# A graph network layer on one core: the node layer of each sum, and the skip layer, in the edge loop

## What is computed

```
h    = relu(layernorm(x))                        # 12500 x 128
sc   = h @ sc weights * node_attr                # skip layer, per node
lin  = h @ lin1 weights * node_attr              # per node
w    = mlp(rbf(dist) * cut(dist))                # 200000 x 128: 8 -> 64 -> 64 -> 128
msg  = tensor_product(w, lin[src], edge_attr)    # 200000 x 256
agg  = segment_sum(msg, dst) / max(count, 1)     # 12500 x 256
l2   = agg @ lin2 weights * node_attr            # 12500 x 128
alpha= tanh(agg @ alpha_w * node_attr)
out  = x + sc + alpha * l2
```

## Time and profile before

| | us |
|---|---|
| median of 3 runs | 2159.24 (2158.75 to 2160.36) |
| the profiled execution | 2159.53 |
| its span, first to last instruction | 2157.6 |
| stage 1, up to the first gather | 110.9 |
| edge loop, first gather to last L1017 | 1969.5 |
| stage 3 and its barrier, from there to the end | 77.2 |

### The profile page before, as it was taken

How to read it: one execution, slowest core, us unless ns; L and a number is a source line. 1 busy time by engine, 2 the same in 40 slices (tenths; PEclk the granted TensorE clock), 3 DMA queues, 4 the chain that set the end, 5 groups by cost and what they waited for, 6 DMA issues and landing times. The chain is left out here.

```text
span 2157.6 us, 33815 instructions
## 1 busy us (share of the span) xinstructions
PE 1692.3 (78%) x7419; PEld 1337.9 (62%) x7419; DVE 1621.2 (75%) x3574; ACT 863.7 (40%) x2388; POOL 1589.6 (74%) x1730
## 2 busy tenths in 40 slices
PE   3867877778777787777877778777787777877778
PEld 2656666666666666666666666666666666666668
DVE  8667777777777777777777777777777777777767
ACT  4733333333333333333333333333333333333345
POOL 7677777777777777777777777777777777777734
PEclk9989999999999999999999999999999999999999
DMA  4922222222222222222222222222222222222249
GB/s 148 274 68 56 56 56 56 55 55 56 56 56 55 55 56 56 56 55 55 56 56 56 55 55 56 56 56 56 55 57 56 56 55 55 57 56 56 56 112 266
DMA packets 249202, 152.25 MB, mean 71 GB/s; under 512 B 145591, under 2 KB 222960, under 8 KB 249184
## 3 DMA queue, kind: packets, MB, share of 16 engines
q0 software_dynamic: 50112, 102.73, 18.3%
q1 hardware_dynamic: 199072, 49.33, 10.3%
HBM read 130.23 MB, written 21.66 MB: 70 GB/s over the span
## 5 line engine op out<-in xcount | busy, mean ns | idle before, releaser
L808 POOL DMA_INDIRECT lin_g<-lin_table,src_ix x1566 | 1480.3, 945 | 487.5 <-issue 487.5
L862 PE MATMUL ps_agg<-msg,onehot 128*128 128x257 f32 x3132 | 742.9, 386 | 236.6 <-DVE agg L1017 236.6
L862 PEld LDWEIGHTS ps_agg<-msg,onehot 128*128 128x128 f32 x3132 | 573.3, 190 | 389.8 <-issue 315.8
L855 PE MATMUL ps_w<-w,h 128*128 128x256 f32 x1566 | 424.8, 407 | 165.4 <-ACT h L908 163.6
L919 ACT ACTIVATE lin_sh<-lin_g,meta 128x128 f32<-128x128 f32 x1566 | 486.0, 389 | 161.5 <-DMA lin_g<-lin_table,src_ix 160.6
L855 PEld LDWEIGHTS ps_w<-w,h 128*128 128x128 f32 x1566 | 336.3, 253 | 300.4 <-ACT h L908 283.7
L983 DVE TENSOR_TENSOR lin_sh<-lin_g,ps_meta 128x576 f32<-128x576 f32 x261 | 196.8, 754 | 422.9 <-DMA lin_g<-lin_table,src_ix 422.8
L901 ACT ACTIVATE h<-ps_h 128x384 f32<-128x384 f32 x261 | 126.7, 486 | 713.7 <-PE ps_h L838 713.7
L988 DVE TENSOR_TENSOR onehot<-iota,ps_meta 128x768 f32<-128x768 f32 x261 | 246.4, 944 | 0.0
L838 PE MATMUL ps_h<-rbf,w 128*128 128x192 f32 x1044 | 214.2, 328 | 3.4 <-DVE rbf L974 3.4
L846 PE MATMUL ps_h<-h,w 128*128 128x384 f32 x522 | 212.3, 489 | 0.0
(11 more groups left out here) (130 smaller groups left out, 981.0 us busy)
## 6 DMA issues: line engine op xcount, KB each, us to landing
lin_g<-lin_table,src_ix POOLq DMA_INDIRECT x1566
xq<-in_x SPq DMA_DIRECT2D x24, 256.0 KB, 3.8
lin_table<-node_out SPq DMA_DIRECT2D x24, 256.0 KB, 3.4
sc_table<-node_out SPq DMA_DIRECT2D x24, 256.0 KB, 3.7
x<-in_x SPq DMA_DIRECT2D x24, 256.0 KB, 3.5
sc<-sc_table SPq DMA_DIRECT2D x24, 256.0 KB, 4.4
out_dram<-new SPq DMA_DIRECT2D x24, 256.0 KB, 3.2
src_ix<-in_src SPq DMA_DIRECT2D x268, 3.0 KB, 1.6
```

Source lines behind the costliest of these rows:

```text
L808: pool.indirect_dma_start(lin_g[:, u, j, :], None, lin_table, bass.IndirectOffsetOnAxis(ap=src_ix[:, u, j:j + 1], axis=0)).then_inc(gather ...
L855: mm = pe.matmul(ps_w[:, 2 * j * P:(2 * j + 2) * P], cols[:, j, :], w3[:], start=True, stop=True)
L862: mm = pe.matmul(ps_agg[:, 0:COLS], onehot[:, u % 2, j, :], msg[:, u % 2, j, :], start=(j == 0), stop=(j == TILES - 1))
```

## The change

- **Stage 2, node layer in the loop.** segment_sum now takes the messages as the stationary operand and the one-hot tile as the moving one: twelve products of 128 columns in place of six of 257, and the sum comes out transposed (ps_sumT). ACT copies it (copy_sums, at the head of each of its steps). PE applies lin2 and alpha to it (node_layer, two accumulated products of 129 columns) and multiplies the edge count with a one. DVE counts edges by a reduction over the one-hot tiles (counts, 768 elements) and accumulates 130 columns instead of 257, one group later and inside `late`, between the messages o11 and o01. The two blocks of `agg` shrink likewise.
- **Stage 2, skip layer in the loop.** In iterations 0 to 48 PE multiplies two blocks of hT with w_sc, ACT scales them, DVE adds x (skip_sum, 256 columns) into an SBUF tile `skip`; SP loads the two operands after a wait for the skip_sum before.
- **Stage 2, the quotient.** cut/dist is no longer formed in stage 1. DVE forms it once an iteration (quotient: a reciprocal of 16x192 and a product) at the end of step u=3; spread_aq at the head of the next step waits for it.
- **Stage 1.** x is loaded first and the statistics start at once; the preparations are spread over the steps; the weights' DMAs are issued by ACT, 28 of them ahead of its first root; rstd is no longer applied by POOL but by ACT as it evacuates. sc_table is gone; hT is stored instead (the same bytes). L644 and the later q product are gone.
- **Stage 3.** One chain forms count, gain and tanh for all nodes at once; then three blocks of a step are scaled and added by DVE, the fourth by ACT and POOL, and the step is stored. No loads, no PE.

The core of the diff:

```
@@ PE, stage 2 @@
 def spread_aq(i):
-    pe.wait_ge(aq_in, 64 * (i + 1))
+    pe.wait_ge(quot_ready, i + 1)
...
-    pe.matmul(ps_rbf[:, 1, 0:SEG], sel_one[:], aq[:, 1, :], start=True, stop=True).then_inc(rbf_spread, 1)
+    pe.matmul(ps_rbf[:, 1, 0:SEG], sel_one[:], quot[:], start=True, stop=True).then_inc(rbf_spread, 1)
...
-def segment_sum(i, u):
+def segment_sum(i, u, skip_pair=None):
+    n = i * SLOTS + u
+    if skip_pair is not None:
+        pe.wait_ge(hT_landed, 16 * (skip_pair + 1))
+        for b in range(2):
+            pe.matmul(ps_sc[:, b * P:(b + 1) * P], hT_in[:, b * P:(b + 1) * P], w_sc[:], start=True, stop=True)
     pe.wait_ge(msg_ready, i * SLOTS + u + 1)
-    pe.wait_ge(agg_ready, i * SLOTS + u + 1)
-    for j in range(TILES):
-        mm = pe.matmul(ps_agg[:, 0:COLS], onehot[:, u % 2, j, :], msg[:, u % 2, j, :], ...)
+    for c in range(2):
+        for j in range(TILES):
+            mm = pe.matmul(ps_sumT[:, c * P:(c + 1) * P], msg[:, u % 2, j, c * P:(c + 1) * P], onehot[:, u % 2, j, :], ...)
     mm.then_inc(sums_ready, 1)
+def node_layer(i, u):
+    n = i * SLOTS + u
+    pe.wait_ge(count_ready, n + 1)
+    pe.wait_ge(sumT_ready, n + 1)
+    pe.wait_ge(w_read, ... n + 2)
+    pe.wait_ge(agg_ready, n + 1)
+    pe.matmul(ps_l2[:, COUNT:COLS], edge_count[:, u % 2, :], one[:], start=True, stop=True)
+    for c in range(2):
+        mm = pe.matmul(ps_l2[:, 0:COUNT], sumT[:, u % 2, c * P:(c + 1) * P], w_lin2[:, c, :], ...)
+    mm.then_inc(l2_ready, 1)
...
 for u in range(SLOTS):
     if u == 0:
         spread_aq(i + 1)
+    node_layer(the group before)
     layer3(i, u + 1)
     segment_sum(i, u)            # layer1, layer2 follow as before
@@ ACT, stage 2 @@
+    copy_sums(i, u)
+    if share and u == 1:
+        scale_sc(...)
     if u == 0:
         sines(i + 1)
@@ DVE, stage 2 @@
+def quotient(i):
+    dve.wait_ge(aq_in, 64 * (i + 1))
+    at_least(dve, rbf_spread, i)
+    dve.reciprocal(quot[:], aq[:, 0, :]).then_inc(recip_done, 1)
+    dve.wait_ge(recip_done, i + 1)
+    dve.tensor_tensor(quot[:], quot[:], aq[:, 1, :], ALU.mult).then_inc(quot_ready, 1)
...
 for u in range(SLOTS):
-    late(i + (u + 1) // SLOTS, (u + 1) % SLOTS)
+    late(i + (u + 1) // SLOTS, (u + 1) % SLOTS, earlier)     # accumulate(earlier) ahead of o01
+    counts(i + (u + 1) // SLOTS, (u + 1) % SLOTS)
     if u == 0:
         fractions(i + 1)
     products(*ahead)
-    accumulate(i, u)
     columns(*ahead)
     if u == 0:
         basis(i + 1)
+    if u == 2 and share:
+        skip_sum(i, ...)
+    if u == 3 and not last:
+        quotient(i + 2)
```

More of the change, by code:

```diff
@@ L109, in window_steps, with blocks @@
     def window_steps(b):
-        return sum(7 if padded(k) else 6 for k in range(b))
+        return sum(5 if padded(k) else 4 for k in range(b))
+    def blocks(n):
+        return NB if n < STEPS else REST
     def parted(table):
@@ L210, in gnn_kernel @@
[L210 to L214, removed]
@@ L265, in _ @@
[L265 to L273, removed]
@@ L274, in _ @@
[L274 to L277, removed]
-                    sp.dma_start(w_lin2[0:HID, 0, 0:MUL], lin2_ws).then_inc(w_edges_in, 16)
-                    sp.dma_start(w_lin2[0:HID, 0, DIM:], alpha_w).then_inc(w_edges_in, 16)
+                    load_x(2)
@@ L450, in product, with turn @@
-                    def product(t, j, blocks=NB):
-                        n, b = t * UNROLL + j, j % 2
+                    def turn(n):
+                        if n <= STEPS:
+                            pe.wait_ge(h_ready, n + 1)
+                            at_least(pe, hT_ready, n - 1)
+                            for k in range(blocks(n)):
+                                last = pe.transpose(psT[:, n % 2, k * P:(k + 1) * P], h[:, n % 2, k, :], ident[:])
+                            last.then_inc(transposed, 1)
@@ L1138, in _ @@
-                    for i in range(IN):
-                        load(i, i)
-                    steps(sp, body)
-                    for b in range(2):
-                        whole = len(range(b, STEPS, 2))
-                        sp.wait_ge(out3[b], 16 * (whole + (REST if b == STEPS % 2 else 0)))
+                    for n in range(STEPS):
+                        sp.wait_ge(low_ready, n + 1)
+                        sp.wait_ge(high_ready, n + 1)
+                        sp.dma_start(node_rows(out, n), result[:, n * NB:(n + 1) * NB, :]).then_inc(out_stored, 16)
@@ L1185, in _ @@
                     dve.wait_ge(scale_ready, 1)
-                    copy_low(0, 0)
-                    steps(dve, body)
-                    update(STEPS, STEPS % IN)
+                    dve.tensor_tensor(pre[:], whole[:, :, ALPHA], scale[:], ALU.mult).then_inc(pre_ready, 1)
+                    dve.wait_ge(alpha_ready, 1)
+                    dve.tensor_tensor(gain[:], alpha[:], scale[:], ALU.mult).then_inc(gain_ready, 1)
+                    dve.wait_ge(gain_ready, 1)
+                    for n in range(STEPS + 1):
+                        for j in range(min(ON_DVE, blocks(n))):
+                            blk, rows = n * NB + j, slice(0, P if n < STEPS else REST_ROWS[j])
+                            last = dve.scalar_tensor_tensor(out=result[rows, blk, :], in0=whole[rows, blk, 0:DIM], scalar=gain[rows, blk:blk + 1],
+                                                            in1=result[rows, blk, :], op0=ALU.mult, op1=ALU.add)
+                        last.then_inc(low_ready, 1)
@@ L1251, in _ @@
+                    act.wait_ge(pre_ready, 1)
+                    act.activation(alpha[:], pre[:], ACT.Tanh).then_inc(alpha_ready, 1)
+                    act.wait_ge(gain_ready, 1)
+                    for n in range(STEPS):
+                        blk = n * NB + ON_DVE
+                        at_least(act, high_ready, n - 1)
+                        act.activation(grown[:, n % 2, :], whole[:, blk, 0:DIM], ACT.Copy, scale=gain[:, blk:blk + 1]).then_inc(grown_ready, 1)
                 @block.gpsimd
```

947 lines of the change are left out of this document (443 added, 504 removed).

## The result

| | before | after |
|---|---|---|
| median (range), us | 2159.78 (2158.75 to 2160.36) | 2460.78 (2458.33 to 2461.51) |
| span | 2157.6 | 2457.7 |
| stage 1, to the first gather | 110.9 | 112.0 |
| loop, to the last accumulate | 1969.5 | 2312.9 |
| stage 3 | 77.2 | 32.8 |

The ratio is 1.139 (95% interval 1.137 to 1.141). The forecast was 2263, its range 2175 to 2345: the direction and the place are right, the time is 198 us too low. By stages the loop cost 343 instead of 168, stage 1 gained nothing instead of 16, stage 3 gained 44 instead of 48.

What follows compares the result with a forecast made beforehand. POOL's issuing of gathers, 30.0 us an iteration, was taken to set the loop's pace. From 2159.5 us, +168 for the loop (45 of it clock), -16 for stage 1 and -48 for stage 3 gave 2263; range 2175 to 2345.

Steps and rivals of the forecast that it cites:

- The added wait: Loop, after the quotient: DVE and PE wait in turn through spread_aq, node_layer and layer3, 3.40 us once an iteration.
- The register load: DVE's step in the loop: no longer hidden behind L983, it costs 0.15 us a group, bounds 0 and 0.68.
- The 0.35 at u=0: Loop, step u=0: late waits on ACT's sine and scale_lin; 0.35 us taken of a computed 0.46.
- The reciprocal: DVE's quotient, once an iteration: reciprocal of 192 columns at 6.0 ns a column, 1.33 us.
- PE's 24 short products: segment_sum on PE in the loop: 24 x 0.116 = 2.78 us, against 2.85 for 12 products of 257 columns.
- rival 4: Weight loads of a group's 24 short products aren't hidden: 250 us more in the loop, total 2510; chance 0.05.
- The clock: TensorE's half clock after idling for the quotient: 0.7 us an iteration, bounds 0 and 1.5, 45 us in all.
- rival 1: Half clock after every quotient on all of the chain: 96 us in place of 45, total 2314; chance 0.18.
- The counts: DVE's reduction of 768 one-hot elements in each group: 0.92 us, bounds 0.67 and 1.1.
- Stage 1: Earlier start, first store near 22 instead of 40: 94 against 110.9 us; -16 taken, bounds -5 and -28.
- Stage 3: After the loop: DVE adds three blocks a step at 0.27 us each; about 29 us against 77.2, so -48.
- Rival 2: The wait is covered and POOL stays the loop's bound: loop +2, total 2098, faster; chance 0.09.

Runs made afterwards that it cites:

- e13: Changed kernel plus 32 TensorE products of 128 columns, read by nothing, after layer2 of step u=3; 3240.2 us beside 3129.9 of the kernel before.
- e9: Changed kernel, quotient at end of u=1, POOL normalising with ones and zeros columns (mean not subtracted); 2101.02 us beside 2161.74 of the kernel before.
- e5: Changed kernel with only quotient(i+2) moved from the end of step u=3 to u=1; 3097.1 us against 3177.2 of the kernel before.

## Why the prediction was wrong, step by step

- **The added wait** was right: place, order, both engines in turn, 3.40 us at full clock (3.30 in e13). The register load was sized 0.15 and costs nothing, its lower bound: o11 (L1041) starts at 1010.83, the accumulate at 1011.10, 0.27 behind it. The 0.35 at u=0 is a wait of 0.25. The reciprocal was 1.33 as worked out, PE's 24 short products 2.68 from start to start (2.78 worked out), so rival 4 falls.
- **The clock** is one of the two mis-sized terms. The step said that three us at half speed cost 1.5 us of work and took 0.7. Both halves failed. The bound asked how much work is lost in 3 us, but the chain has 3.3 us of work at full clock and takes nearly twice that at half: 2.65 more. And the row it was read from, the stretch at 0.50 that began 1.7 us after PE resumed, came after an idle time of 2.97; here PE idles 5.12 us and the clock had in nearly every stop fallen before it resumed, in the one shown 2.5 us before. 64 x (2.65 - 0.7) = 125 us. Even rival 1, which had the clock pay every time, priced it at 1.5. The Trainium skill (TensorE: Matmul & The Clock Gate, HAM oscillation) says that idle gaps in a loop bring the half clock in every turn; the trace agrees, with 0.50 to 0.55 over the chain behind each of the 64 quotients.
- **The counts** were scaled by elements from a reduction whose inner step is 128 bytes: 0.72 for 576, so 0.92 for 768. Measured 1.40, with a step of 512 bytes, beyond my upper bound of 1.1. That alone is 64 x 4 x 0.48 = 123 us, as much as the clock. The register load's 0.15 and some 0.06 elsewhere came back, so a group's step was 6.53 in place of 6.26, 64 x 4 x 0.27 = 69 us. The row was of the right operation and nearly the size, but of another stride; the Trainium skill (SBUF — State Buffer, Door 1: The DMA port swizzle) says that each access that crosses into another line of 16 bytes pays, but gives no price. By that rule 128 and 512 bytes would cost the same; here they are 1.40 and 1.92 ns an element, against 1.23 for neighbours (the reduction at 1.40 takes three elements into one, the two others six, so it differs in more than the stride).
- Together the iteration adds up to 4 x 6.53 + 0.91 + 0.33 + 1.71 + 5.95 + 0.25 = 35.3, and from k_turn to k_turn it is 35.4 (with a skip pair). Without the clock's 2.65 and the stride's 2.0 it would be 30.7. That both gains would show in the time is arithmetic, no run has it. The two missed terms, 125 and 69, less 19 are the loop's 175: the wait at u=0 was 0.10 smaller (6), the chain at full clock 3.30 and not 3.40 (6), the stops average 5.89 and not 5.95 (4), and start and end, with what the last iteration saves, cost 6 and not 9 (3).
- **Stage 1**: I worked out ACT's queue (first store 24.6, predicted 22) and the bytes, but kept POOL's four operations a step at their price before, though their form changed. With 0.71 instead of 0.44, POOL bounds the stage: 112.0 instead of 94. With the cheap form it is 94.1 to 92.0, near the predicted value. 18 us.
- **Stage 3**: blocks cost 0.33 instead of 0.27 on DVE, 4 us.
- **The range** ended at 2345 by less than its own bounds. The register load's 0.53 in three or four steps of 64 iterations is 102 to 136 us and not 70, and the upper bound of the counts, 1.1 for 0.92, another 46, which the range left out.
- **Rivals.** Rival 1's condition came true, half clock after every quotient, at nearly twice its price. Rival 2 didn't come true in this kernel, but by e9 an early quotient gives what it named, POOL as the bound, at 2101 (2098 worked out). DVE alone needs 4 x 6.53 + 0.91 + 0.33 + 1.71 = 29.1 us, less than POOL's 30.0 even with the dear counts.

## What to carry to other kernels

Ask of each value that one engine hands to another in an in-order queue how long before its use it can be made: here the loop lost 343 us with two instructions at the end of one step and 3 us with the same two, two steps earlier. When a chain on TensorE runs after an idle time like the 5.12 us here, price all of it at half clock, not part of it by what a row elsewhere shows. Take an instruction's price only from a row with the same operation, stride and operand form, and recheck each engine that a stage's new bytes and queues leave nearest its limit.

## What the runs showed of the hardware

- DVE's reduction of 768 float32 elements to 128: 0.94 us over neighbours, 1.47 over elements 512 bytes apart.
- POOL's operation on 128x128 float32: product and sum of two columns 0.45 us (median), subtraction and maximum or sum with a number 0.71, subtraction and maximum with a column 0.79.
- TensorE's granted clock fell to half (1.2 GHz) around each idle time of 5.12 us in the loop, 2.0 to 5.3 us after the last product, and came back 4.8 to 8.2 us after PE had resumed; it stayed at 1.00 in the stop of e13 shown above, where 64 instructions had filled most of the wait. A chain of 3.30 us took 5.95 at half.
- A register load from SBUF on DVE, behind instructions that ran without a wait, cost nothing: the accumulate behind it started 0.27 after the instruction before it. In the kernel before it cost 0.27 behind an instruction that had waited for a DMA.
- In e5's loop TensorE stood idle for over 4 us 79 times, 8.8 us at the median. In the case shown the products that ACT's copy of the sums (L932) waits for are recorded as done at 1041.23, but the copy starts only at 1049.23, and TensorE behind it. No instruction in the records explains the delay; what it is wasn't found:

```profile
1041.72 0.81 PE L821 MATMUL ps_h<-h,w 128*128 128x384 f32 x2
1049.23 0.38 ACT L932 ACTIVATE sumT<-ps_sums 128x256 f32<-128x256 f32 x1 [13.76 <-remote]
1049.72 0.56 PE L855 MATMUL ps_w<-one,edge_count 128*128 128x1 f32 x2 [7.19 <-issue]
```
